# Output projections one step sooner in the last attention group, late row turnings in one bank, and quarter sums shared by GpSimd and VectorE

## What is computed

```
x = layernorm(x + self_attention(x))       # 32 heads of 16, int4-quantised inputs and weights
x = layernorm(x + x @ attention(ctx).T)    # attention(ctx): 512x512 softmax matrix per batch
x = layernorm(x + ffn(x))

self_attention: result, ch_bias = chunk_decompose(x)    # 64-row chunks, per-chunk channel bias and scales
                Q, K, V = projections; probs = softmax(Q K^T); ctx = probs V
                r2, cb2 = chunk_decompose(ctx); out = r2 @ WO + cb2 @ o_weight.T + o_bias
ffn:            a = act_quant(fwht(x)); gate = a @ Wg; up = a @ Wu     # 512 -> 2048, ternary weights
                h = silu(gate) * up; out = act_quant(fwht(h)) @ Wdown
```

## Time and profile before

| what | value |
|---|---|
| median of 3 runs | 1156.97 us (1153.02 to 1161.09) |
| the profiled execution: its time / its span | 1161.64 us / 1159.7 us |
| TensorE matmuls busy | 950.7 us, 82% |
| VectorE busy | 880.4 us, 76% |
| ScalarE busy | 660.8 us, 57% |
| GpSimd busy | 386.9 us, 33% |
| mean granted TensorE clock | 0.94 of full speed |

### The profile page before, as it was taken

The page is one execution under the profiler, slowest core; times in us unless marked ns, Lnnn a source line. Parts: engine busy times, 40 slices in busy tenths (PEclk is TensorE's granted clock), DMA queues, the critical chain, the costliest instruction groups (busy, mean ns, idle before and its releaser), DMA issues. The chain is left out here.

```text
span 1159.7 us, 13393 instructions
## 1 busy us (share of the span) xinstructions
PE 950.7 (82%) x4075; PEld 365.5 (32%) x4128; DVE 880.4 (76%) x1634; ACT 660.8 (57%) x1091; POOL 386.9 (33%) x299
## 2 busy tenths in 40 slices
PE   3657699889998888888987869896989799878765
PEld 1223222222222222222222334343434344433322
DVE  7996588888889988998897379658656775677347
ACT  3777467777777677766665234355424542365252
POOL 4103366556666775572201413150005000500000
PEclk9788799999999999999999988998999999999977
DMA  9865545655566454545342212330333023202400
GB/s 333 332 244 194 179 147 165 184 172 178 184 183 184 149 164 139 183 140 172 125 127 78 97 73 55 64 100 1 64 81 110 1 50 87 46 1 64 109 9 36
DMA packets 90684, 145.00 MB, mean 125 GB/s; under 512 B 12339, under 2 KB 52147, under 8 KB 89078
## 3 DMA queue, kind: packets, MB, share of 16 engines
q1 hardware_dynamic: 90614, 144.16, 41.2%
HBM read 84.75 MB, written 42.21 MB: 109 GB/s over the span
## 5 line engine op out<-in xcount | busy, mean ns | idle before, releaser
L1393 DVE TENSOR_REDUCE neg_max<-banks 128x1 f32<-128x512 f32 x512 | 331.5, 683 | 47.1 <-PE banks L1232 43.6
L1350 ACT ACTIVATE probs<-banks 128x512 f32<-128x512 f32 x512 | 278.7, 599 | 124.1 <-PE banks L1253 123.4
L1138 POOL TENSOR_TENSOR rstd<-vare,half 128x1 f32<-128x1 f32 x48 | 28.1, 586 | 411.9 <-DVE vare L1130 411.9
L1267 PE MATMUL banks<-probs,v_st 128*32 128x512 f32 x1024 | 138.2, 612 | 17.7 <-ACT pv_z L1363 16.6
L1806 PE MATMUL banks<-q_T,f_int_all 128*128 128x512 bf16 x493 | 124.0, 393 | 17.9 <-DVE h_ring L1827 11.3
L1232 PE MATMUL banks<-attn_T,x_T 96*128 96x512 bf16 x256 | 99.5, 398 | 11.6 <-DVE neg_max L1393 10.2
L1232 PE MATMUL banks<-k_st,q_st 96*128 96x512 bf16 x256 | 98.4, 384 | 6.7 <-DVE neg_max L1393 5.9
L1253 PE MATMUL banks<-x_T,attn_T 99*128 99x512 bf16 x256 | 99.5, 389 | 5.4 <-DMA x_T<-nm_T 2.5
L1253 PE MATMUL banks<-q_st,k_st 99*128 99x512 bf16 x256 | 97.1, 388 | 7.7 <-ACT probs L1350 6.0
L1821 ACT ACTIVATE h_ring<-h_ring 128x512 f32<-128x512 f32 x64 | 40.3, 630 | 104.1 <-DVE h_ring L1816 104.0
L1816 DVE TENSOR_TENSOR h_ring<-banks,gate_row 128x512 f32<-128x512 f32 x64 | 44.1, 689 | 59.6 <-PE banks L1806 58.8
(11 more groups left out here) (276 smaller groups left out, 1616.2 us busy)
## 6 DMA issues: line engine op xcount, KB each, us to landing
f_int_all<-in_ffn_dram SPq DMA_DIRECT2D x24, 512.0 KB, 7.5
qk_parts<-parts SPq DMA_DIRECT2D x32, 384.0 KB, 2.5
woT<-in_ffn_dram SPq DMA_DIRECT2D x24, 512.0 KB, 3.5
qk_parts<-parts SPq DMA_DIRECT2D x32, 256.0 KB, 2.9
pv_rows<-pv_z SPq DMA_DIRECT2D x32, 256.0 KB, 5.2
hz<-h_turned SPq DMA_DIRECT2D x32, 256.0 KB
x_T<-qk_parts SPq DMA_DIRECT2D x16, 384.0 KB, 4.1
attn_T<-qk_parts SPq DMA_DIRECT2D x16, 384.0 KB, 5.1
```

Source lines behind the costliest of these rows:

```text
L1267: last = pe.matmul(pv_bank[32 * j:32 * j + 32, :], v_st[g.v][:, kt].rearrange("p h d -> p (h d)")[:, (HD + 1) * head:(HD + 1) * head + 2 * ...
L1350: act.activation(probs[ktp][:, j, i, :], st_bank[(16 * g.n + 2 * w + i) % STB], ACT.Exp).then_inc(exp_done, 2)
L1393: dve.tensor_reduce(neg_max[:, g.h, tile:tile + 1], s_bank[(16 * g.n + tile) % SB], AX.X, ALU.max, negate=True).then_inc(max_done, 1)
```

## The change

1. `O_LAST_AT`: projections 0 and 1 move from step 1 to step 0, projection 2 from step 2 to 3, projection 3 from step 3 to 4. `DVE_O_AT`: VectorE's first tile moves from step 1 to step 0; tiles 1 to 3 stay at 3, 5, 7. In the last group all four steps of `dve_nm` are issued in step 0, ahead of that tile.
2. The turnings move from steps 4, 5, 6 and the tail's first step to steps 6 and 7 and the tail's steps w = 6 and 7, all into `s_bank[1]`; they wait for `o_read` 2, and each for the copy of the one before (`x1_T_sb`, already in `pe_x1_T`). ScalarE's copies move with them.
3. `make_y4` is split in `make_y4a` and `make_y4`. For batch 0 GpSimd makes the first step of all four tiles and VectorE the second; `pool_norm` of piece 14 follows tile 1 instead of tile 0; VectorE's second step of tile t-1 stands after the statistics of tile t; `dve_quant1` of tile 1 stands ahead of the last second step; the two `dve_extreme` of piece 14 move behind `dve_quant1` of tile 3. For batches 1 to 3 GpSimd issues the same instructions in the same order.

```diff
--- before.py
+++ after.py
@@ -1206,7 +1206,8 @@
             LAG = 5
 
             PV_AT, QK_AT, V_AT, HIGH_AT, MIDDLE_AT = (1, 2, 6, 7), (3, 5), 5, (4, 6), (5, 7)
-            O_LAST_AT, TURN_LAST_AT, DVE_O_AT = {1: (0, 1), 2: (2,), 3: (3,)}, {4: 0, 5: 1, 6: 2}, (1, 3, 5, 7)
+            O_LAST_AT, TURN_LAST_AT, DVE_O_AT = {0: (0, 1), 3: (2,), 4: (3,)}, {6: 0, 7: 1}, (0, 3, 5, 7)
+            TURN_END_AT = {6: 2, 7: 3}
 
             def v_bank(kt):
                 return (psum[4], psum[5], psum[6], psum[3])[kt]
@@ -1312,9 +1313,8 @@
                                 need(pe, "o_read", n + 1 - SB)
                             pe_o(pe, 0, n, s_bank[n % SB])
                     if g.last and u in TURN_LAST_AT:
-                        n = TURN_LAST_AT[u]
-                        need(pe, "o_read", n + 2)
-                        pe_x1_T(pe, 0, n, s_bank[(n + 1) % SB])
+                        need(pe, "o_read", 2)
+                        pe_x1_T(pe, 0, TURN_LAST_AT[u], s_bank[1])
                     if g.r == 7 and g.b and u in (3, 7):
                         pe.wait_ge(nm_T_ready, g.n + 1)
                         if u == 3:
@@ -1376,8 +1376,7 @@
                         if u in MIDDLE_AT:
                             act_middle(act, g.tile(2), MIDDLE_AT.index(u))
                     if g.last and u - 1 in TURN_LAST_AT:
-                        n = TURN_LAST_AT[u - 1]
-                        act_x1_T(act, 0, n, s_bank[(n + 1) % SB])
+                        act_x1_T(act, 0, TURN_LAST_AT[u - 1], s_bank[1])
                     if g.b > 1 and g.r == 3 and 1 <= u <= 4:
                         act_round(act, g.b - 2, u - 1)
                     if u == 3 and g.n < PIECES:
@@ -1411,8 +1410,11 @@
             def dve_period(dve, g):
                 for u in range(8):
                     for i in range(2):
-                        if u < 2 and 2 * u + i < 4:
+                        if u < 2 and not g.last:
                             dve_nm(dve, g, 2 * u + i)
+                        if u == 0 and g.last:
+                            dve_nm(dve, g, 2 * i)
+                            dve_nm(dve, g, 2 * i + 1)
                         if not g.last:
                             dve_max(dve, g + 1, 2 * u + i)
                     if u == 2:
@@ -1571,8 +1573,8 @@
                     for w in range(8 - LAG, 8):
                         for i in range(2):
                             pe_scores_T(pe, last_group, w, i)
-                        if w == 8 - LAG:
-                            pe_x1_T(pe, 0, KD - 1, s_bank[KD % SB])
+                        if w in TURN_END_AT:
+                            pe_x1_T(pe, 0, TURN_END_AT[w], s_bank[1])
                         if w in (5, 6):
                             pe_pv(pe, last_group, w - 5)
                     for kt in (2, 3):
@@ -1590,7 +1592,9 @@
                         act_exp(act, last_group, w)
                         if w == 8 - LAG:
                             act_pv(act, last_group + -1)
-                            act_x1_T(act, 0, KD - 1, s_bank[KD % SB])
+                            act_x1_T(act, 0, 1, s_bank[1])
+                        if w in TURN_END_AT:
+                            act_x1_T(act, 0, TURN_END_AT[w], s_bank[1])
                     act_pv(act, last_group)
 
                 @block.vector
@@ -1689,12 +1693,15 @@
                     last = eng.tensor_tensor(d[:, s], r[:, 0], r[:, 1], op)
                 return last
 
-            def make_y4(eng, B, t):
+            def make_y4a(eng, B, t):
                 i = 4 * B + t
                 need(eng, "x2_ready", i + 1)
                 need(eng, "y4", i)
                 need(eng, "scaled2", 4 * (B - 1))
                 did(butterfly(eng, y4a[:], x2[:, B % 2, t, :], 1), "y4a")
+
+            def make_y4(eng, B, t):
+                i = 4 * B + t
                 need(eng, "y4a", i + 1)
                 need(eng, "t2_mm", i)
                 did(butterfly(eng, y4[:], y4a[:], 2), "y4")
@@ -2208,11 +2215,15 @@
                 B = b + 1
                 pool_rstd(pool, 1, 4 * B)
                 pool_rstd(pool, 1, 4 * B + 1)
+                make_y4a(pool, B, 0)
                 make_y4(pool, B, 0)
                 pool_rstd(pool, 1, 4 * B + 2)
+                make_y4a(pool, B, 1)
                 make_y4(pool, B, 1)
                 pool_rstd(pool, 1, 4 * B + 3)
+                make_y4a(pool, B, 2)
                 make_y4(pool, B, 2)
+                make_y4a(pool, B, 3)
                 make_y4(pool, B, 3)
 
             with nc.Block() as block:
@@ -2270,9 +2281,8 @@
                 def _(pool):
                     for t in range(KD):
                         pool_rstd(pool, 1, t)
-                        if t < KD - 1:
-                            make_y4(pool, 0, t)
-                        if t == 0:
+                        make_y4a(pool, 0, t)
+                        if t == 1:
                             pool_norm(pool, 14, rs_bc)
                     pool_norm(pool, 15, rs_bc)
                     for b in range(NB - 1):
@@ -2291,15 +2301,17 @@
                         dve_xm(dve, 0, t, xm_bank(t))
                         if t == 1:
                             dve_recip(dve, 15)
+                        if t:
+                            make_y4(dve, 0, t - 1)
                         dve_xm_norm(dve, 0, t)
                         if t == 2:
                             dve_quant1(dve, 0, 0)
+                    dve_quant1(dve, 0, 1)
                     make_y4(dve, 0, KD - 1)
-                    for t in range(1, KD):
+                    for t in range(2, KD):
                         dve_quant1(dve, 0, t)
-                        if t == 1:
-                            for which in range(2):
-                                dve_extreme(dve, 14, which)
+                    for which in range(2):
+                        dve_extreme(dve, 14, which)
                     dve_tok1(dve, 0)
                     for b in range(NB - 1):
                         dve_first(dve, b)
```

## The result

The changed kernel takes 1150.39 us (median of 20 runs, 1147.09 to 1156.16), the kernel before 1158.2 us (median of 20 runs, 1153.02 to 1163.72). The ratio is 0.9936 with a 95% interval of 0.9921 to 0.9951: faster by 0.6%, some 7.4 us. Forecast was 1148.8 us, 8.2 us less than before, with eight chances in ten for 1144 to 1155.

A forecast was written before the change was run, and what follows sets the result against it. No engine was full; chains of waits bound the attention tail and the next block's quarter sums. Gains of 5.0 + 3.2 = 8.2 us took the profiled 1161.64 to 1153.4, the median to 1148.8 us; eight in ten: 1144 to 1155.

The forecast's parts named there:

- Projections sooner: Last attention group: nm_T copy 3.0 us sooner, TensorE late for the first scores, exponentials 2.0 us sooner.
- Turnings late: Last group's tail, listed step by step: waits for z go, waits for ScalarE's copies come; block ends 5.0 us sooner.
- Quarter sums: Next block up to the first gate matmul: quant1 of tile 1 sooner, 3.2 us gained, range 0 to 4.5.
- The reduces ahead of the gate scales: End of the quarter sums: two extremes ahead of dve_tok1 delay the first gate matmul by 0.6 us.
- Behind 681.8 the work moves as a whole: 0: From the first gate matmul on, everything shifts together; no further gain or loss, batches 1 to 3 included.
- Half clock eats part of it: Rival, both stretches: TensorE's half clock leaves gains of 1.5 + 3.2 or 5.0 + 0, 1152 us; chance 0.18.
- wrong: Signs against the forecast: granted clock under 0.8 in the tail or behind 674; gap before first gate matmul unchanged.
- Not held: Quarter sums: tile 3's second step does not wait for GpSimd's pool_norm 15; gain 4.0 us instead of 3.2.
- more than forecast: Rival: second step not held, clock full, PV quarters hide; 10.5 us gained or a little more, 1145.5 us; chance 0.15.
- the quarter sums do not do what they say: Rival: VectorE's four second steps, each held by GpSimd, become the chain; gain there 0 to 1, 1151.5 us; chance 0.12.
- Slower: Rival: half clock from the first late turning through the gate chunks costs 11.7 us against 8.2, 1160.5 us; chance 0.05.
- No change can be told from one of about 1%: Whole time: differences within about 1% (11.6 us) cannot be told from no change; the forecast lies within that.

The follow-up runs named there:

- e3: Kernel before with only the earlier projections, maxima steps and first tile in the last group, turnings as before: last group 27.81 us, ratio 0.9969.
- e1: Kernel before with only the last-group edits (projections and turnings), quarter sums as before: last group 25.79 us, quarter sums 33.54 us, ratio 0.9941.
- e12: Changed kernel plus 16 idle matmuls in the quarter sums: last group 25.78 us, quarter sums 29.58 us, ratio to the kernel before 0.9878.
- e5: Changed kernel with GpSimd's multiply of piece 15 waiting for VectorE's last second step: last group 25.79 us, quarter sums 28.81 us, ratio to before 0.9929.
- e7: Changed kernel with waiting multiply 15, the two reduces behind the gate scales, and idle matmuls in both stretches: 25.79 and 28.39 us, ratio to before 0.9885.
- e4: Kernel before with only the turnings late and in one bank, projections as before: last group 29.53 us, quarter sums 33.53 us, ratio 0.9975.
- e6: Changed kernel with waiting multiply 15 and the two reduces behind the gate scales: last group 27.36 us, quarter sums 29.34 us, ratio to before 0.9911.
- e9: Same program as e6 (changed kernel, waiting multiply, reduces moved), run again: last group 27.37 us, quarter sums 30.64 us, ratio to before 0.9881.

## Why the prediction was right, point by point

- **Projections sooner.** The `nm_T` copy was forecast 3.0 us sooner and came 2.93 sooner. TensorE, not the transfer, was forecast to be late for the last group's first scores, by 1.1 us. Measured from the cast, those scores start at 618.83 - 609.75 = 9.08 instead of 626.54 - 615.21 = 11.33, 2.25 sooner where I had 2.0, and the row of 618.83 has no wait for the transfer. Confirmed, and e3 shows the step by itself.
- **Turnings late.** The waits for z went; turning 1 waits 0.61 us for the copy, forecast 0.65. The stretch gained 4.73, forecast 5.0. At equal (full) clock it is 30.74 - 25.79 = 4.95. The sum was right by luck in part, for two things in it were not: my step-by-step list ends 27.1 us behind the cast without any half clock, where a full-clock execution takes 25.79, since I let the handovers cost too much (the exponentials of w = 2, w = 6 and w = 7 start 0.4, 1.1 and 1.3 us sooner in e1 than in the list); and it was set against a kernel before that lost 1.35 us to half clock (32.09 against 30.74). The two cancel.
- **Quarter sums.** Here a term was mis-sized: "Against 681.77 the gain is 3.2 us". Measured 2.70. The mechanism (quant1 of tile 1 ahead of the last half sums) is right, and so is the hold: forecast 2.1 us from the end of GpSimd's step (669.7 on its axis) to the end of the pair, measured 1.84 (659.22 to 661.06). (Of the rows that the prediction had for such a hold only the sum of 1.03 us reads two tensors in SBUF, the norm of 1.48 us reads one; the pair of half sums is itself of the first kind.) What failed is the comparison: the changed block was listed at full clock, the one before stood in the trace with a Hadamard of 2.08 us at half clock. At one clock the edit is worth 1.96. In the profiled run the changed kernel lost 1.25 us to half clock of its own, which the range had (0 to 4.5) and the term had not. My list was 0.7 us too slow as well (30.3 against the 29.58 of e12), which hid part of it. Over both parts: at one clock the edit is worth 4.95 + 1.96 = 6.9 us. The forecast of 8.2 took 3.3 us of the old kernel's half clock for gain and lost 2.0 us of it to the slow lists.
- **The reduces ahead of the gate scales** were priced at 0.6 us; e5 against e7 gives 0.42.
- **"Behind 681.8 the work moves as a whole: 0".** Nearly. VectorE's first product with the gate came 2.21 us sooner relative to the block's start, not 2.70, because the first gate matmuls ran at half clock (granted clock 0.51 in their first microsecond). Over the rest of the program nothing can be read: kernels with the very same code behind this point (e1, e3, e4) take 475.0, 475.0 and 478.2 us for it in their profiles.
- **Rivals.** "Half clock eats part of it" was partly true. Both signs that were named as "wrong" came, a granted clock under 0.8 in the tail (0.72) and in the quarter sums (0.57), and the forecast held all the same: they were no signs, because the kernel before had them too and lost more in the same places (0.58 over 8 us, 0.52 over 7). "Not held", a part of "more than forecast", is refuted by the 1.81 us. Of "the quarter sums do not do what they say" the holds are half there: two of VectorE's four second steps are held, 1.32 and 1.81 us long, the others take 0.69 and 0.76. Its gain of 0 to 1 us is refuted by the 1.96 at full clock. "Slower" needed half clock through both stretches and the gate; the changed kernel's stretches (27.36 and 30.83) are together 7 us under those of the profile before and 4 us under the 30.74 and 31.54 that the old code shows at full clock.
- **"No change can be told from one of about 1%".** It could: the ratio's interval, 0.9921 to 0.9951, tells 0.6% from nothing. Single terms of this size it does not tell; those rest on the stretches.

## What to carry to other kernels

When a forecast is made by setting a hand-made list against a trace, list the old kernel in the same way first: the half clock, the handovers and the holds that are in the trace's number but not in the list otherwise pass for gain. Look at the granted clock of the stretch in both, and compare kernels at the same clock. When VectorE gets the second half of a job from GpSimd, look what GpSimd does next: here a long multiply right behind the handover began first and VectorE waited it out; one wait on GpSimd gave 0.8 us in the stretch, too little to be read from the whole time.

## What was unexpected of the hardware

The same code of the last group showed TensorE at full clock throughout the tail in some executions (e1, e5, e12: 25.78 to 25.79 us) and at half clock for some 3.4 us of it in others (changed, e6, e9: 27.36 to 27.37), with nothing in between, though the wait ahead of turning 1 was 0.61 us in e1 as in the changed kernel. e5 and e6 ran on one chip. And in the quarter sums TensorE kept full clock in all four kernels whose waits idle matmuls filled, and in one of ten without. Why the unfilled executions differ among themselves is not settled by these runs.

One hold was left as it is: GpSimd's multiply 14 also held VectorE's half sums of tile 1 (1.32 us instead of 0.76), without cost, since TensorE came to that turning later; moving it was not tried.
